# Feed-forward network in five 128-token tiles per pair of images instead of six, with the left-over tokens collected over pairs

## The chip, the cores and the metric

One Trainium2 chip, one of its cores. The metric is the device time of one execution in microseconds (us), the median of several runs. Engines are called as the profile calls them: PE (matmul), PEld (weight load of PE), DVE (vector), ACT (scalar), POOL (GpSimd), SP (which here only issues DMAs).

## What is computed

Thirty-two images of 224 x 224 x 3 go through a tokenizer, an attention block and a feed-forward network (FFN); all of it is float32 but the two matmuls of the FFN, whose operands are rounded numbers held exactly in bf16. Cut to what matters here:

```python
# tokenizer: two embeddings of 16x16 patches, five depthwise 3x3 convolutions with a pointwise one
# each, layer norm; 196 tokens an image, one class token before, 128 text tokens behind: T = 325
h = concat([cls, layernorm(tokenizer(x)), txt], axis=1)      # 32 x 325 x 192
# attention: q, k, v are small MLPs of layernorm(h), a query sees the 64 keys before it
h = h + layernorm(scores @ v)
# FFN, token by token (D = 192, H = 512)
t = layernorm(h)
u, g = split(bitlinear(t, w_in, g_in))                       # 192 -> 2 x 512
out = h + bitlinear(gelu(g) * u, w_out, g_out)               # 512 -> 192
# bitlinear(x): rmsnorm, scale by the row's maximum, round, multiply by weights of -1, 0, 1
```

Everything behind the attention works on a token by itself, so it does not matter there which tokens share a tile of 128 partitions.

## The kernel before, in words

The work goes in 16 pairs of images. An image has 325 tokens, held in three tiles of 128, 128 and 69 rows (`ROWS`); a pair has `NT` = 6 tiles, and row n of the list `(0..2)` is the first image, `(3..5)` the second. Each engine has one function `turn(it, par, on)`, which is an order written out by hand: for turn `it` it issues one piece of the youngest pair's embedding, pieces of the older pairs' convolutions, attention and FFN, up to six pairs deep. `all_turns` calls it for 22 turns. So in the steady state a turn of each engine holds the work of one pair, taken from five or six different pairs, and the only thing that sets the order of an engine is its `turn`.

The pieces that matter here:

- `embed_chunk(pair, m, ks)` (L389 inside) multiplies x by the weights, 18 float32 matmuls of 392 columns a pair. SP's `load_x` brings the next pair's x when the last one has been used.
- `square` (L367 to L372) and `mlp` (L419 to L424) are the pointwise convolutions and the six projections' matmuls.
- `transposes(a, t)` (L431) turns the normalised tokens of tile t of both images, packed side by side in `xh`, into columns `xT`: three PE transposes a tile.
- `mixed_values(a, i)` (L472 to L478) makes the attention's output, three units a pair. Unit 1 is the third tile (69 rows) of the two images: four matmuls of 192 columns, two for each image.
- The FFN of a tile n of pair f: `round_tokens` (ACT), `rounded_token_transposes` (PE, L491, 2 transposes), `rounded_tokens` (ACT), `ffn_in` (PE, L501, 4 bf16 matmuls of 512 columns), `gate_tanh` (ACT), `gated` and `lifted` (DVE, L1383 and L1402), `hidden_scale` (POOL), `mean_square` (ACT), `hidden_root` (POOL), `hidden_round` (DVE, L1161 to L1174), `round_hidden` (ACT), `rounded_hidden_transposes` (PE, L513, 4 transposes), `rounded_hidden` (ACT), `ffn_out` (PE, L522, 4 bf16 matmuls of 192 columns), `finished` (DVE, L1392), `store` (SP). There is one buffer for nearly all of it, so tiles follow each other through a chain of engines.
- Before the first tile of a pair, `hidden_bn` (L1316), `token_scale_0` to `token_scale_3` and `token_gain` on DVE make the scales of all six tiles at once.

A float32 matmul is two PE instructions in the trace (the two passes follow each other), a transpose or a bf16 matmul is one.

## Time and profile before

| | |
|---|---|
| median of 3 runs | 1230.72 us (1226.99 to 1232.67) |
| the profiled execution | 1227.0 us, its span 1225.1 us |
| mean granted clock of TensorE | 0.959 of full speed |
| busy: PE, PEld | 1122.0 us (92%), 853.2 us |
| busy: DVE, ACT, POOL | 1038.1 us (85%), 966.7 us (79%), 813.9 us (66%) |
| DMA | 40.25 MB, 9.2% of the 16 engines' time |
| PE's share of the chain that ended last | 81% |

The page of the profile gives, for each group of instructions, the busy time, the mean of one, and how long the engine stood idle before it and for whom. Its second part cuts the span in 40 slices: PE is busy in all but the first four and the last eight or so, and the granted clock is full (9) until the last two. The page's averages are taken over stages with different limits, so the prediction reads stretches of the time line.

### The profile page before, as it was taken

Reading aid. Unit: us, or ns where it says so; the run is one execution under the profiler, and the core shown is the slowest. Engines: PE = TensorE matmul, PEld = TensorE weight load, DVE = VectorE, ACT = ScalarE, POOL = GpSimd, SP = SyncE. Lnnn points to the kernel's source line nnn. Section 1 sums busy time; section 2 is a strip of 40 time slices with the busy share of each in tenths; the row PEclk is TensorE's granted clock in tenths of the full one; section 3 lists DMA queues with packets and bytes.
Section 4 is the critical chain, followed back from the end, with each engine's and each line's share of the span. In section 5 each row is a group of like instructions: output and inputs, shape, how many; then the busy total and the mean of one; then the engine's idle time right before and its main releaser. Section 6 shows DMA issues by size and latency. Waiting matters only on the chain.

```text
span 1225.1 us, 19501 instructions
## 1 busy us (share of the span) xinstructions
PE 1122.0 (92%) x5617; PEld 853.2 (70%) x5674; DVE 1038.1 (85%) x3012; ACT 966.7 (79%) x2437; POOL 813.9 (66%) x860
## 2 busy tenths in 40 slices
PE   6777999999999999999999999999999998889544
PEld 3555777777777777777777777777877766566322
DVE  1887598999999999999999999999999998866643
ACT  4556677989898988979898989889798978776543
POOL 4454576776877867777768778677777686755421
PEclk9998999999999999999999999999999999999655
DMA  8111010101010010101010100101010000000000
GB/s 320 40 47 40 8 40 7 49 14 49 5 49 15 16 49 15 49 12 49 13 50 5 45 19 16 49 15 49 12 49 13 11 6 19 6 19 11 12 11 10
DMA packets 21513, 40.25 MB, mean 33 GB/s; under 512 B 2656, under 2 KB 18208, under 8 KB 19104
## 3 DMA queue, kind: packets, MB, share of 16 engines
q1 hardware_dynamic: 21408, 39.01, 9.2%
q8 instruction: 46, 0.75, 0.3%
q14 instruction: 59, 0.48, 0.1%
HBM read 31.02 MB, written 7.99 MB: 32 GB/s over the span
## 4 chain that ended last, share of the span: by engine, by line
PE 81%; ACT 6%; DVE 6%; POOL 4%; issue 2%; DMA 1%; SPq 0%; DVEq 0%; POOLq 0%; ACTq 0%
PE bank L389 14%; PE bank L419 6%; PE bank L420 6%; PE bank L501 6%; PE bank L367 4%; PE bank L368 4%; PE bank L422 3%; PE bank L424 3%; PE bank L423 3%; PE bank L513 3%; PE bank L522 3%; PE bank L443 2%; PE bank L444 2%; PE bank L370 2%; PE bank L371 2%
## 5 line engine op out<-in xcount | busy, mean ns | idle before, releaser
L1212 DVE SCALAR_TENSOR_TENSOR bank<-padA,c_col,bank 128x406 f32<-128x406 f32 x560 | 357.8, 639 | 7.8
L389 PE MATMUL bank<-x_sb,w_emb 128*128 128x392 f32 x576 | 215.3, 500 | 11.4 <-ACT padA L746 7.3
L801 ACT ACTIVATE prod<-padB,c_col 128x196 f32<-128x196 f32 x432 | 181.3, 448 | 33.9 <-DVE padB L1233 31.1
L1692 POOL TENSOR_TENSOR yg<-y_f,c_gout 128x512 f32<-128x512 f32 (+1 forms) x96 | 121.8, 1268 | 109.8 <-DVE y_f L1402 109.8
L389 PEld LDWEIGHTS bank<-x_sb,w_emb 128*128 128x128 f32 x576 | 102.8, 191 | 63.7 <-ACT padA L746 9.2
L801 ACT ACTIVATE early<-padB,c_col 128x196 f32<-128x196 f32 x288 | 124.1, 452 | 1.9 <-POOL accB L1723 1.4
L1685 POOL TENSOR_TENSOR s<-s,c_mhalf 128x1 f32<-128x1 f32 (+1 forms) x96 | 53.0, 552 | 84.3 <-ACT s L877 84.3
L1383 DVE SCALAR_TENSOR_TENSOR ya<-th,bank 128x512 f32<-128x512 f32 (+1 forms) x96 | 65.6, 683 | 48.7 <-ACT th L870 48.1
L501 PE MATMUL bank<-w_in,xq 128*128 128x512 bf16 (+1 forms) x327 | 93.3, 404 | 8.7 <-ACT xq L864 5.7
L858 ACT ACTIVATE yq<-bank 128x512 bf16<-128x512 f32 (+1 forms) x96 | 50.8, 530 | 56.9 <-PE bank L513 56.5
L870 ACT ACTIVATE th<-bank,sm 128x512 f32<-128x512 f32 (+1 forms) x96 | 65.4, 681 | 24.7 <-PE bank L501 24.0
L513 PE MATMUL bank<-c_id,r 128*128 128x128 f32 (+1 forms) x384 | 56.3, 273 | 29.0 <-DVE y_f L1402 26.4
L1392 DVE SCALAR_TENSOR_TENSOR o_sb<-bank,dq,h 128x192 f32<-128x192 f32 (+1 forms) x96 | 39.6, 412 | 44.4 <-PE bank L522 44.4
L367 PE MATMUL bank<-accA,w_sq 128*128 128x196 f32 x256 | 65.9, 339 | 11.6 <-DVE accA L1212 5.3
L501 PEld LDWEIGHTS bank<-w_in,xq 128*128 128x128 bf16 (+1 forms) x384 | 39.4, 105 | 52.9 <-issue 16.5
L513 PEld LDWEIGHTS bank<-c_id,r 128*128 128x128 f32 (+1 forms) x384 | 44.6, 150 | 43.4 <-ACT r L850 37.3
L850 ACT ACTIVATE r<-yg,s 128x512 f32<-128x512 f32 (+1 forms) x96 | 68.7, 716 | 5.1 <-DVE s L1174 4.5
L864 ACT ACTIVATE xq<-bank 128x256 bf16<-128x256 f32 (+1 forms) x96 | 34.0, 354 | 45.8 <-PE bank L491 44.5
L419 PE MATMUL bank<-xT,w_sq 128*128 128x325 f32 x192 | 68.9, 440 | 0.7 <-ACT xT L760 0.7
L420 PE MATMUL bank<-xT,w_sq 128*128 128x325 f32 x192 | 68.2, 436 | 0.0
L1708 POOL TENSOR_TENSOR prod<-prod 128x392 f32<-128x392 f32 x48 | 48.8, 1017 | 29.0 <-ACT prod L801 29.0
L1685 POOL TENSOR_TENSOR sm<-sm,c_mhalf 128x6 f32<-128x6 f32 x32 | 43.7, 1366 | 36.0 <-DVE sm L1358 35.2
(224 smaller groups left out, 3461.2 us busy)
## 6 DMA issues: line engine op xcount, KB each, us to landing
x_sb<-xt SPq DMA_DIRECT2D x16, 1176.0 KB, 5.4
out<-o_sb SPq DMA_DIRECT2D x64, 96.0 KB
w_sq<-squares SPq DMA_DIRECT2D x1, 3840.0 KB, 16.4
h_sb<-txt SPq DMA_DIRECT2D x32, 51.8 KB
out<-o_sb SPq DMA_DIRECT2D x32, 51.8 KB
h_sb<-txt SPq DMA_DIRECT2D x32, 44.2 KB
w_in<-win SPq DMA_DIRECT2D x1, 1024.0 KB, 18.1
c_row<-broads SPq DMA_DIRECT2D x1, 672.0 KB, 19.2
```

Source lines behind the costliest of these rows:

```text
L367: mm(dstA[img], w[:, AA, :], chunks[img], start=True, stop=False)
L389: done = mm(pE[:, 0:2 * N_PATCH], w_emb[:, k, m, :], x_sb[:, k, :], start=k == 0, stop=k == KC - 1)
L419: mm(dst, w[:, AA, :], src[:, c, :], start=True, stop=False)
L420: mm(dst, w[:, B0A + c, :], src[:, 2, :], start=False, stop=True).then_inc(at_full, 1)
L501: done = mm(dst[0:m, :], xq[:, c, 0:m], w_in[:, c, half * HID:(half + 1) * HID], start=c == 0, stop=c == 1)
L513: done = nc.tensor.transpose(pUP[:, c * P:c * P + m], r2[0:m, c * P:(c + 1) * P], c_id[0:m, 0:m])
L801: made = go(grid(prod[ACC[s] ^ 1][:, k, :]), tap_view(padB[min(s, 2)], SIDE, k), ACT.Copy, scale=tapcol(s, 1, k))
L850: go(r2[0:m, :], yg[0:m, :], ACT.Copy, scale=s2[0:m, 6:7], bias=MAGIC).then_inc(r2_ready, 1)
L1212: v.scalar_tensor_tensor(grid(acc if k == TAPS - 1 else run), tap_view(pad, ROWS_A, k), tapcol(s, 0, k), grid(run), ALU.mult, ALU.add).the ...
L1383: v.scalar_tensor_tensor(ya[0:m, :], th[0:m, :], 1.0, pGT[0:m, :], ALU.add, ALU.mult).then_inc(f_y, 1)
L1685: return g.tensor_tensor(ap, ap, c_mhalf[0:m, 0:n], ALU.pow)
L1692: g.tensor_tensor(yg[0:m, :], y_f[0:m, :], c_gout[0:m, :], ALU.mult).then_inc(f_yg, 1)
```

## The change

Of an image's 325 tokens, 256 fill two tiles, 64 more go into one half of a third tile that the two images of a pair share (tile 2), and 5 are left. So a pair has five FFN tiles of 128 rows and 10 tokens left over. These 10 rows of `h2` are copied by two DMAs a pair (`hold`) into a side tile `h_side`, which is run through the FFN as a sixth tile of pair 11 (120 rows, pairs 0 to 11) and of pair 15 (40 rows, pairs 12 to 15). FFN tiles: 96 before, 82 after.

```diff
+FFN_TILES = 5
+SIDE_PAIRS = (11, PAIRS - 1)
+LEFT = T - 2 * P - DB
+HELD = 2 * LEFT
+TOK_ROWS = [P] * 5 + [DB + LEFT]
...
+def n_tiles(pair):
+    return FFN_TILES + side(pair)
+def tile_no(pair, n):
+    return pair * FFN_TILES + (pair > SIDE_PAIRS[0]) + n
+def rows(pair, n):
+    return P if n < FFN_TILES else HELD * len(members(group(pair)))
...
 # SP: store of a tile
+                if n == FFN_TILES:
+                    for i, pair in enumerate(members(group(f))):
+                        for img in range(2):
+                            lo = i * HELD + img * LEFT
+                            sp.dma_start(out[pair * 2 + img, T - LEFT:T, :], at[lo:lo + LEFT, :]).then_inc(done, 16)
+                elif n == 2:
+                    for img in range(2):
+                        sp.dma_start(out[f * 2 + img, 2 * P:2 * P + DB, :],
+                                     at[img * DB:(img + 1) * DB, :]).then_inc(done, 16)
...
+            def hold(f, par):
+                sp.wait_ge(h2_ready, f + 1)
+                lo = (f - members(group(f))[0]) * HELD
+                for img in range(2):
+                    sp.dma_start(h_side[group(f)][lo + img * LEFT:lo + (img + 1) * LEFT, :],
+                                 h2[par][img * DB:img * DB + LEFT, TILES + 2, :]).then_inc(held[f % 2], 16)
...
 # PE: the transposes of the third tiles
+            def tail_transposes(a):
+                both = pT[(U_XT + 2) % 2][:, 0:2 * P].rearrange("p (i n) -> p i n", i=2)
+                feat = pT[(U_XT + 2) % 2][:, 2 * P:3 * P]
+                pick = c_id[0:TOK_ROWS[5], :].rearrange("p (i n) -> p i n", i=2)[:, :, 0:LEFT]
+                mm(both[:, :, 0:DB], xh[:, 2, 0:P], c_id[:, :].rearrange("p (i n) -> p i n", i=2), start=True, stop=True)
+                mm(both[:, :, DB:DB + LEFT], xh[0:TOK_ROWS[5], 2, D:D + P], pick, start=True, stop=True)
+                for img in range(2):
+                    o = slice(img * DB, (img + 1) * DB)
+                    mm(feat[o, 0:DB], xh[:, 2, P:D], c_id[:, o], start=True, stop=True)
+                for img in range(2):
+                    o = slice(img * DB, (img + 1) * DB)
+                    done = mm(feat[o, DB:DB + LEFT], xh[0:TOK_ROWS[5], 2, D + P:2 * D],
+                              c_id[0:TOK_ROWS[5], img * DB:img * DB + LEFT], start=True, stop=True)
...
 # PE: unit 1 of the mixed values
+                if i == 1:
+                    half = [slice(img * DB, (img + 1) * DB) for img in range(2)]
+                    for img in range(2):
+                        mm(pT[u % 2][half[img], 0:D], sc1[:, img, P:P + DB], v_sb[:, 1, img, :], start=True, stop=False)
+                    for img in range(2):
+                        mm(pT[u % 2][half[img], 0:D], sc2[0:n2, img, 0:DB], v_sb[0:n2, 2, img, :], start=False, stop=True)
+                    for img in range(2):
+                        done = mm(pT[u % 2][img * DB:img * DB + LEFT, D:2 * D], sc2[0:n2, img, DB:DB + LEFT],
+                                  v_sb[0:n2, 2, img, :], start=True, stop=True)
-                    else:
-                        mm(dst, sc2[0:n2, img, :], v_sb[0:n2, 2, img, :], start=True, stop=False)
-                        done = mm(dst, sc1[:, img, P:P + n2], v_sb[:, 1, img, :], start=False, stop=True)
...
 # DVE: the scales of a pair; with a side tile they wait for the copies
+                if tiles[-1] == NT - 1 and side(f):
+                    for p in range(2):
+                        dve.wait_ge(held[p], (f + 1) // 2 * 32)
...
 # POOL: h2 is not written before it was copied
+                    pool.wait_ge(held[f % 2], f // 2 * 32)
```

The text tokens are loaded with six DMAs a pair instead of four (64 of them go into tile 2, 5 into tile 5). Every step that counted tiles as `f * NT + n` counts them as `tile_no(f, n)`. And the `turn` functions of all five engines are written in a new order; the functions they call are the same, with `if side(...)` around the steps of a sixth tile. Three places of it follow.

PE, one steady turn: the mixed values (L472 to L478) and the transposes of the third tiles (the last L431 row). Before:

```order
L491 MATMUL bank<-c_id,r 128x69 x2
L389 MATMUL bank<-x_sb,w_emb 128x392 x2
L501 MATMUL bank<-w_in,xq 69x512 x4
L477 MATMUL bank<-v_sb,sc 69x192
L478 MATMUL bank<-v_sb,sc 69x192
L477 MATMUL bank<-v_sb,sc 69x192
L478 MATMUL bank<-v_sb,sc 69x192
...
L431 MATMUL bank<-c_id,xh 128x128 x3
L522 MATMUL bank<-w_out,yq 128x192 x4
L431 MATMUL bank<-c_id,xh 128x69 x3
```

And of the change, the same stretch:

```order
L595 MATMUL bank<-c_id,r 128x128 x2
L568 MATMUL bank<-v_sb,sc 64x192 x2
L570 MATMUL bank<-v_sb,sc 64x192 x2
L572 MATMUL bank<-v_sb,sc 5x192 x2
L605 MATMUL bank<-w_in,xq 128x512 x4
...
L527 MATMUL bank<-c_id,xh 128x128 x3
L508 MATMUL bank<-c_id,xh 128x2x64
L509 MATMUL bank<-c_id,xh 128x2x5
L512 MATMUL bank<-c_id,xh 64x64 x2
L515 MATMUL bank<-c_id,xh 64x5 x2
```

Four matmuls of 69 output rows have become six, of 64, 64 and 5 rows, and three transposes have become six matmuls.

DVE, the second pair at the program's start: the last taps of its convolution F1 (L1212) and the statistics of the first pair's tokens (L1270), before:

```order
L1212 SCALAR_TENSOR_TENSOR bank0<-padA2,c_col,bank0 128x406 x6
L1270 BN_STATS st_a<-h_sb 128x6 x2
L1270 BN_STATS st_a<-h_sb 69x6
L1270 BN_STATS st_a<-h_sb 128x6 x2
L1270 BN_STATS st_a<-h_sb 69x6
```

```order
L1315 SCALAR_TENSOR_TENSOR bank0<-padA2,c_col,bank0 128x406 x5
L1315 SCALAR_TENSOR_TENSOR accA0<-padA2,c_col,bank0 128x406
L1373 BN_STATS st_a<-h_sb 128x6 x5
L1373 BN_STATS st_a<-h_sb 69x6
```

The last tap, which writes `accA0` for PE, stood behind the statistics and now stands ahead of them.

SP, the end of its queue of the change (before, it ends with six stores of one DMA each for every pair):

```order
L380 DMA h_side<-h_1 5x192 x2
L373 DMA out<-o_sb 128x192
L369 DMA out<-o_sb 64x192 x2
L373 DMA out<-o_sb 128x192 x4
L369 DMA out<-o_sb 64x192 x2
L373 DMA out<-o_sb 128x192 x2
L366 DMA out<-o_sb 5x192 x8
```

The two copies of the last pair stand ahead of its stores, and the last store is eight DMAs of five rows.

## Rows read from the trace of the kernel before

**Rows 1.** busy time of each engine in stretches (columns: stretch; its us; busy us, instructions)

```profile
105.00:172.00 67.00, 67.00 (x318) 53.41 (x317) 47.77 (x113) 47.21 (x122) 34.55 (x41) 0.99 0.12 40
...
914.70:982.00 67.30, 67.09 (x350) 52.17 (x353) 63.32 (x187) 59.39 (x151) 49.95 (x53) 1.00 0.04 11
982.00:1049.60 67.60, 59.04 (x312) 44.40 (x314) 60.77 (x187) 56.81 (x141) 50.35 (x50) 1.00 0.04 12
1170.00:1225.00 55.00, 25.85 (x89) 11.86 (x88) 19.42 (x55) 21.05 (x48) 10.86 (x12) 0.50 0.03 10
```

**Rows 2.** time line of PE, FFN tiles in a steady turn (start us; busy us; instruction)

```profile
638.64 0.41 PE L513 MATMUL bank<-c_id,r 69*128 69x69 f32 x4
638.89 0.76 PE L422 MATMUL bank<-xT,w_sq 128*128 128x325 f32 x2
...
657.54 0.29 PE L491 MATMUL bank<-c_id,r 69*128 69x69 f32 x2
657.67 0.76 PE L419 MATMUL bank<-hq,w_sq 128*128 128x325 f32 x2
...
658.82 1.02 PE L501 MATMUL bank<-w_in,xq 128*69 128x512 bf16 x4
659.68 0.71 PE L422 MATMUL bank<-hq,w_sq 128*128 128x325 f32 x2
...
666.06 0.60 PE L513 MATMUL bank<-c_id,r 128*128 128x128 f32 x4
666.49 0.71 PE L419 MATMUL bank<-hk,w_sq 128*128 128x325 f32 x2
...
667.59 0.49 PE L522 MATMUL bank<-w_out,yq 128*128 128x192 bf16 x4
667.92 1.51 PE L389 MATMUL bank<-x_sb,w_emb 128*128 128x392 f32 x4
669.27 0.38 PE L491 MATMUL bank<-c_id,r 128*128 128x128 f32 x2
669.49 0.71 PE L422 MATMUL bank<-hk,w_sq 128*128 128x325 f32 x2
```

**Rows 3.** the same time line: mixed values unit 1, transposes, narrow matmuls

```profile
683.08 0.29 PE L457 MATMUL bank<-q,k 128*69 128x69 f32 x2
683.21 0.54 PE L456 MATMUL bank<-q,k 128*128 128x191 f32 x2
...
690.27 0.49 PE L477 MATMUL bank<-v_sb,sc 69*69 69x192 f32 x2
...
691.58 0.49 PE L472 MATMUL bank<-v_sb,sc 128*128 128x192 f32 x2
...
698.93 0.35 PE L431 MATMUL bank<-c_id,xh 69*128 69x69 f32 x3
699.12 1.53 PE L389 MATMUL bank<-x_sb,w_emb 128*128 128x392 f32 x4
```

**Rows 4.** time line at the start, DVE

```profile
99.24 1.65 DVE L1270 BATCH_NORM_STATS2 st_a<-h_sb 128x6 f32<-128x192 f32 x6 [4.91 <-DMA h_sb<-cls]
...
101.73 0.63 DVE L1212 SCALAR_TENSOR_TENSOR accA<-padA,c_col,bank 128x406 f32<-128x406 f32 x1
```

**Rows 5.** time line at the start, PE

```profile
102.46 0.99 PE L367 MATMUL bank<-accA,w_sq 128*128 128x196 f32 x2 [3.32 <-DVE accA L1212]
```

**Rows 6.** time line of the end: DVE's statistics of pairs 13 and 15

```profile
1047.86 1.65 DVE L1316 BATCH_NORM_STATS2 st_f<-h 128x6 f32<-128x192 f32 x6
...
1156.39 1.66 DVE L1316 BATCH_NORM_STATS2 st_f<-h 128x6 f32<-128x192 f32 x6 [0.98 <-POOL h L1751]
```

**Rows 7.** line 1392 on DVE (ns min/median/max, first and last start us, forms)

```profile
L1392 DVE SCALAR_TENSOR_TENSOR o_sb<-bank,dq,h x96: 403/415/420, 215.0 to 1222.2; 128x192 f32<-128x192 f32 x64, 69x192 f32<-69x192 f32 x32
```

**Rows 8.** SP's issues of line 320 (ns min/median/max, first and last start us)

```profile
L320 SPq DMA_DIRECT2D h_sb<-txt x6: 362/705/2042, 607.4 to 743.0; - x6
```

**Rows 9.** the page's DMA issues (KB each, median us to landing)

```profile
x_sb<-xt SPq DMA_DIRECT2D x16, 1176.0 KB, 5.4
```

More of the change, by code:

```diff
@@ L151, in build @@
         sm = [sb(f"sm{i}", [P, 12, NT]) for i in range(2)]
+        h_side = [sb(f"h_side{i}", [P, D]) for i in range(2)]
         w_g = sb("w_g", [P, NT, D])
@@ L329, in turn @@
             def turn(it, par, on):
+                if on[6]:
+                    store(it - 6, 3)
+                    if side(it - 6):
+                        store(it - 6, 4)
+                if on[3]:
+                    load_cls(it - 3)
+                if on[6]:
+                    store(it - 6, n_tiles(it - 6) - 1)
+                if on[5]:
+                    store(it - 5, 0)
                 if on[0]:
@@ L494, in ffn_in @@
             def ffn_in(f, n):
-                m = ROWS[n % TILES]
-                pe.wait_ge(f_xq, f * NT + n + 1)
-                if not (first(f) and n < 2):
-                    pe.wait_ge(f_yq, f * NT + n - 1)
+                m = rows(f, n)
+                pe.wait_ge(f_xq, tile_no(f, n) + 1)
+                if not (tile_no(f, n) < 2):
+                    pe.wait_ge(f_yq, tile_no(f, n) - 1)
                 for half, dst in ((0, pUP), (1, pGT)):
@@ L516, in ffn_out @@
             def ffn_out(f, n):
-                m = ROWS[n % TILES]
-                pe.wait_ge(f_yq, f * NT + n + 1)
-                if not (first(f) and n == 0):
-                    pe.wait_ge(f_out, f * NT + n)
+                m = rows(f, n)
+                pe.wait_ge(f_yq, tile_no(f, n) + 1)
+                if not (tile_no(f, n) == 0):
+                    pe.wait_ge(f_out, tile_no(f, n))
                 for c in range(4):
@@ L607, in turn @@
                     ffn_out(it - 5, 0)
+                if on[1]:
+                    embed_chunk(it - 1, EMB_GA, range(4, 6))
                 if on[4]:
@@ new lines, in turn @@
+                if on[5]:
+                    if side(it - 5):
+                        round_tokens(it - 5, odd, 5)
+                    rounded_tokens(it - 5, 4)
+                if on[1]:
+                    products(it - 1, L_, range(7, 8))
+                    products(it - 1, L_, range(8, 9))
+                    mix_out(it - 1)
+                if on[3]:
+                    mlp_out(it - 3, U_K1, hk, "kb1", ACT.Gelu, 1)
+                if on[5]:
+                    gate_tanh(it - 5, 4, odd)
@@ new lines, in turn @@
+                if on[3]:
+                    mlp_out(it - 3, U_V1, hv, "vb1", ACT.Gelu, 1)
+                if on[2]:
+                    products(it - 2, F3_, range(1, 2))
+                    products(it - 2, F3_, range(2, 3))
+                if on[3]:
+                    mlp_out(it - 3, U_V1, hv, "vb1", ACT.Gelu, 2)
+                if on[2]:
+                    products(it - 2, F3_, range(3, 4))
+                    products(it - 2, F3_, range(4, 5))
+                if on[5]:
+                    if side(it - 5):
+                        rounded_tokens(it - 5, 5)
@@ new lines, in turn @@
+                if on[3]:
+                    queries_out(it - 3, 1)
+                if on[5]:
+                    if side(it - 5):
+                        rounded_hidden(it - 5, 4)
+                if on[1]:
+                    loc_out(it - 1)
+                if on[4]:
+                    round_tokens(it - 4, par, 1)
+                    rounded_tokens(it - 4, 0)
+                if on[3]:
+                    queries_out(it - 3, 2)
+                if on[0]:
+                    products(it, G_, range(3, 4))
@@ L1313, in hidden_bn @@
                     dve.wait_ge(h2_ready, f + 1)
-                for n in tiles:
-                    m = ROWS[n % TILES]
-                    done = v.bn_stats(st_f[0:m, n, :], h2[par][0:m, n, :])
+                if tiles[-1] == NT - 1 and side(f):
+                    for p in range(2):
+                        dve.wait_ge(held[p], (f + 1) // 2 * 32)
+                for n in range(tiles[0], min(tiles[-1] + 1, n_tiles(f))):
+                    m = rows(f, n)
+                    done = v.bn_stats(st_f[0:m, n, :], hidden(f, par, n))
                 if tiles[-1] == NT - 1:
@@ new lines, in turn @@
+                if on[2]:
+                    taps(it - 2, F3_, 3)
+                if on[5]:
+                    if side(it - 5):
+                        lifted(it - 5, 5)
+                if on[2]:
+                    taps(it - 2, F3_, 4)
+                if on[1]:
+                    if first(it - 1):
+                        ternary_weights()
+                if on[2]:
+                    taps(it - 2, F3_, 5)
+                    taps(it - 2, F3_, 6)
+                if on[5]:
+                    hidden_round(0, it - 5, n_tiles(it - 5) - 1, odd)
```

1071 lines of the change are left out of this document (524 added, 547 removed).

## The prediction

> **What bounds the kernel now.** I read the stretches first, then single pieces of PE's time line, then the two ends. From 105 us on PE is busy in every microsecond: 67.00 of 67.00 us, and still 67.09 of 67.30 us before 982 us, at the full granted clock, 1.00, which is the 2.4 GHz level [rows 1]. In the same stretches DVE, the next engine, has 63.32 of 67.30 us to do [rows 1]. One turn of the program, the work of one pair, takes some 67.4 us here. So for 877 us, 13 turns, the time is the number of microseconds that PE streams, and what DVE, ACT and POOL save is worth nothing. Behind 982 us this ends: PE has 59.04 and DVE 60.77 of 67.60 us, and in the last 55 us PE works 25.85 us at a granted clock of 0.50, the 1.2 GHz level [rows 1]: only FFN tiles are left, one after the other. There, and at the start, waits decide. The change has to be priced by these two rules: PE's streaming in the middle, the chain at the ends.
>
> **FFN tiles on PE.** The price of a piece is the start of what follows it less its own start, since matmuls overlap by their tails. A 128-row tile: hidden transposes 666.49 - 666.06 = 0.43 us, output matmuls 0.33, token transposes 0.22 [rows 2], and input matmuls 659.68 - 658.82 = 0.86 us, which have 512 columns however many rows the tile has. Together 1.84 us. A 69-row tile: 0.25 + 0.33 (the same 192 columns) + 0.13 + 0.86 = 1.57 us [rows 2]. A pair had 4 x 1.84 + 2 x 1.57 = 10.50 us and has 5 x 1.84 = 9.20 us: **-1.30 us a turn**. A sixth of the tiles goes, but only an eighth of their PE time, and what goes were the cheap ones. FFN tiles run from 215 us on (DVE's first `finished` [rows 7]), so up to 982 us this is worth 767 / 67.4 = 11.4 turns, -14.8 us. The side tile of pair 11 stands where that pair's sixth tile stood, with 120 rows for 69: +0.3 us, in the stretch where PE is no longer full; I leave it out.
>
> **Mixed values, unit 1.** Four matmuls of 192 columns take 691.58 - 690.27 = 1.31 us, 0.327 us each, of two passes [rows 3]. Now there are six, because each image's 69 queries are cut in 64 and 5, and a matmul of 5 output rows streams the same 192 columns. The rows show that 69 or 128 output rows make no difference and that each float32 matmul starts when the one before has streamed; by that six cost 1.96 us, **+0.65 us a turn**. Below, the two matmuls of each couple write different partitions (0 to 63, 64 to 127); if they streamed wholly side by side, the unit would cost 3 x 0.327 = 0.98 us, -0.33. I take +0.65, the value that the rows show, and keep the other end for the range. 13 turns: +8.5 us.
>
> The Trainium skill speaks for the other end: "TensorE: Matmul & The Clock Gate", Part 3 on packing small matmuls, has three matmuls with 32 output rows each on column tiles of their own run 2.38 times as fast as one after the other. Nothing in this trace uses such tiles. It is my first rival.
>
> **Transposes of the third tiles.** Three transposes of 69 columns, one pass each, take 699.12 - 698.93 = 0.19 us [rows 3]. They become six ordinary float32 matmuls, two passes each: one of 128 columns (a pass of 128 columns is 0.11 us, half of the two token transposes [rows 2]), 0.22 us; one of 10; two of 64; two of 5. A 69-column matmul costs 683.21 - 683.08 = 0.13 us for two passes [rows 3]. Four passes of 64 columns are thus 0.24 us. The six passes of 5 or 10 columns cost between 0.04 us (by their columns) and 0.39 us (as much as 69 columns, if loading the weights sets a least time); the nearest row is a 69-column pass, so I take 0.38. Sum 0.84 us, **+0.65 us a turn** (from +0.3), 13 turns: +8.4 us.
>
> So in the middle the change gives -14.8 + 8.5 + 8.4 = **+2.1 us**: what the FFN saves on PE, the attention's pieces pay back.
>
> **The start.** The last tap of the second pair's convolution F1 now stands ahead of the statistics on DVE. Before, it was queued behind them, they waited 4.91 us for a DMA, and PE waited 3.32 us for the tap [rows 4, 5]. That wait goes. What is late next are the transposes that need those statistics, which had hidden behind F1's matmuls. Bounds 0 and -3.3 us; I take -2.0 us. The rest of DVE's order at the start is the same.
>
> **The end.** From pair 13's statistics to pair 15's are 1156.39 - 1047.86 = 108.5 us for two pairs, 54.3 us a pair [rows 6], with 12 FFN tiles in them. If the FFN's chain alone set this, a tile would be worth 9.0 us; if the last pair's attention does, nothing. Pairs 12, 13 and 14 each lose a tile. DVE's share (60.77 of 67.60 us [rows 1]) says that both are near; I take a third, 2.7 us a tile, **-8 us**. Pair 15 keeps six tiles. Against that stand: pair 15's own unit 1 and transposes, now on the chain, +1.3 us; its side tile's statistics wait for `h2`, an SP issue and a landing, where the sixth tile's `h2` was ready, +0.8 us; and the last store is eight DMAs where it was one. SP needs 0.36 us for an issue at the least [rows 8], so seven more are 2.5 us, of which part lies beside the first ones' landing: +2.0 us. Net -3.9 us (from -20 to +4). The 24 DMAs of the first side tile (some 9 us of SP) come behind 982 us, with no x left to load; I cost them at nothing, their cover being the one tile that may pass before `o_sb` is needed again.
>
> Nothing is taken for the two copies a pair, the two more text loads (DMA's share is under a tenth), or for the work saved on DVE, ACT and POOL in the middle: PE's streaming covers it all.
>
> **Sum:** +2.1 - 2.0 - 3.9 = -3.8 us against the profiled execution's 1227.0 us, so 1223.2 us. That execution is at the low end of the runs; the median is 3.7 us above it, and I put the change's median as much above its own: **1226.9 us**. A measurement of this kernel tells about 0.5%, 6.2 us, from no change: faster is below 1224.6, slower above 1236.9.
>
> **Rivals.**
> *The couples stream together (faster).* Within a couple the second matmul's first pass can run beside the first matmul's second pass, and so on through the unit: 12 passes of 0.163 us take the time of 7, 0.82 us less a turn; in the transposes 8 narrow passes take the time of 5, 0.18 us less. 13 turns: -13.0 us, 1213.9 us. For it: the couples are written next to each other, image by image, onto different partitions. Against: nothing in this trace does it, and between their two passes they are in one order.
> *A change of the array's shape stops PE (slower).* The program has only full-width matmuls now. The change brings in widths of 64 and 32 output rows. If PE must finish one width before it starts the next, each change shows the tail that is hidden today: a float32 couple of passes is busy 0.49 us where the next starts after 0.33 [rows 3], so 0.16 us. Three changes in unit 1 and two in the transposes make 0.8 us a turn, 13 turns +10.4 us: 1237.3 us; if the weight load is not hidden either, up to 10 us more. It decides from 0.1 us a change on. The Trainium skill states this rule: "TensorEngine Tiling (Array Packing)", Key Properties, says that changing the tiling mode drains TensorE. No row of this trace shows it.
> *Both at once:* 1226.9 - 13.0 + 10.4 = 1224.3 us.
> *The new order makes PE wait for x (slower).* Behind the last use of a pair's x, PE now has the transposes of a third tile, G and W2 (14 matmuls of 196 columns, 0.33 us each), four of 325 columns (0.55 each) and half an FFN tile, some 9 us, before it needs the next pair's x; before, some five projections' pieces more stood between. The load lands 5.4 us after its issue [rows 9], so it holds unless SP is late by over 3 us behind a store. If each turn lost 1 us: 1240 us.
>
> **How the numbers follow.** Forecast as summed 0.28, together 0.25, both 0.17, shape alone 0.20, a wait in the new order 0.10. Each case spreads by some 6 us, by the end's bounds above all. Faster by over 0.5%: 0.10 + 0.24 + 0.09 = 0.43. Slower: 0.01 + 0.01 + 0.13 + 0.05 = 0.20. The rest, 0.37, within. The range goes from the first rival less 2 us, 1212, to the shape rival plus 5 us, 1242. The likeliest case alone spans 1220 to 1233.
>
> **What would show it.** PE stays full from 105 us to 982 us, with a turn of 67.5 us (forecast), 66.5 (together), 68.3 (shape). Unit 1's starts: 1.96 us to the next piece, or 1.14; gaps of 0.16 us and more ahead of the first 64-row and the first 128-row matmul for the shape rival. The third transposes: 0.84 us. Pair 13 to pair 15 in some 103 us. From DVE's last `finished` (start 1222.2 before [rows 7], the span's end 2.9 us later) to the end some 5 us. I am wrong if PE shows idle time in the middle, or if the end moves by more than 8 us.

## The result, and the profile after

| | before | after |
|---|---|---|
| median | 1231.53 us (4 runs, 1226.99 to 1232.67) | 1209.33 us (4 runs, 1208.73 to 1211.12) |
| ratio | | 0.9829, 95% interval 0.9801 to 0.9857 |
| profiled execution, span | 1227.0, 1225.1 us | 1211.1, 1209.3 us |
| mean granted clock | 0.959 | 0.952 |
| busy PE, PEld | 1122.0, 853.2 us | 1117.2, 843.2 us |
| busy DVE, ACT, POOL | 1038.1, 966.7, 813.9 us | 990.9, 926.1, 786.5 us |
| DMA | 40.25 MB | 40.36 MB |

The change is 1.7% faster. I had forecast 1226.9 us and a range of 1212 to 1242: the time lies below the range, and 4.6 us below my fastest rival. The stretches of the changed kernel, columns as in [rows 1]:

```profile
105.00:172.00 67.00, 66.94 (x333) 52.44 (x332) 49.05 (x115) 46.88 (x121) 33.87 (x37) 0.99 0.11 40
914.70:982.00 67.30, 67.11 (x367) 52.80 (x366) 63.74 (x185) 57.88 (x148) 50.06 (x52) 1.00 0.04 12
982.00:1049.60 67.60, 60.64 (x320) 45.45 (x319) 56.63 (x179) 53.06 (x130) 44.67 (x46) 0.95 0.04 13
1170.00:1209.30 39.30, 16.52 (x59) 7.74 (x58) 13.07 (x37) 13.68 (x30) 7.23 (x8) 0.50 0.04 11
```

Up to 982 us PE is as full as before: the middle is still PE's. So the question is how long a turn is. A good clock for that is SP's load of x, once a pair: SP issues it when PE has read the last of the pair's x. That place is not the same in the two orders, so what lies ahead of the sixth load and behind the last one can shift by some us from one to the other; the length of ten turns can't. The sixth and the last load (start us, us) of the kernel before:

```profile
228.54 0.35 SPq L304 DMA_DIRECT2D x_sb<-xt  x1
...
903.05 0.35 SPq L304 DMA_DIRECT2D x_sb<-xt  x1
```

and of the changed kernel:

```profile
227.91 0.35 SPq L356 DMA_DIRECT2D x_sb<-xt  x1
...
892.51 0.34 SPq L356 DMA_DIRECT2D x_sb<-xt  x1
```

Ten turns took 674.51 us and take 664.60: 67.45 and 66.46 us each. Against the kernel before, the changed one has gained 0.6 us up to the sixth load, 9.9 us in the ten turns, and 5.3 us from the last load to the end (322.05 and 316.79 us): 15.8 us in all, the difference of the spans. The 0.6 us is understated: up to 60 us this execution had a granted clock of 0.91, the kernel before 0.97. Experiments 3, 6 and 11, whose kernels differ from the changed one there only in a few matmuls of a turn, had 0.97 and their sixth load at 224.8 to 225.6 us, some 3 us ahead of the kernel before.

On PE's time line, a steady turn, unit 1 of the mixed values (L568 to L572) and the third tiles' transposes (L508 to L515) read:

```profile
616.04 0.38 PE L595 MATMUL bank<-c_id,r 128*128 128x128 f32 x2
616.35 0.55 PE L568 MATMUL bank<-v_sb,sc 128*64 128x192 f32 x4
616.73 0.50 PE L570 MATMUL bank<-v_sb,sc 69*64 69x192 f32 x4
617.16 0.50 PE L572 MATMUL bank<-v_sb,sc 69*5 69x192 f32 x4
617.59 1.04 PE L605 MATMUL bank<-w_in,xq 128*128 128x512 bf16 x4
...
627.14 0.39 PE L508 MATMUL bank<-c_id,xh 128*128 128x128 f32 x2
627.36 0.29 PE L509 MATMUL bank<-c_id,xh 69*128 69x10 f32 x2
627.58 0.34 PE L512 MATMUL bank<-c_id,xh 128*64 128x64 f32 x4
627.74 0.24 PE L515 MATMUL bank<-c_id,xh 69*64 69x5 f32 x4
627.91 0.44 PE L595 MATMUL bank<-c_id,r 128*128 128x128 f32 x2
628.18 0.50 PE L444 MATMUL bank<-accA,w_sq 128*128 128x196 f32 x2
```

Unit 1's six matmuls, twelve passes, take 617.59 - 616.35 = 1.24 us, less than the four (eight passes) before took (1.31 us [rows 3]). I had 1.96. The transposes take 627.91 - 627.14 = 0.77 us; I had 0.84. The same unit in a window 0.06 us wide shows how the first couple begins:

```profile
616.15 0.27 PE L595 MATMUL bank<-c_id,r 128*128 128x128 f32 x1
616.35 0.38 PE L568 MATMUL bank<-v_sb,sc 128*64 128x192 f32 x2
```

Two passes stand in 0.38 us, which is what one lasts: they begin 7 ns apart, one for each image. The next two follow after 0.21 us, the later pairs after 0.16. And the two transposes of L595, 0.22 us elsewhere in the turn, hold PE for 616.35 - 616.04 = 0.31 us ahead of the 64-row matmuls and 628.18 - 627.91 = 0.27 us behind them: each change of width leaves a gap. Both of my rival mechanisms are there at once, the first stronger than I had it.

At the start the wait that I had struck out is still there, with another releaser (PE; before, it was 3.32 us for DVE's tap at 102.46 [rows 5]):

```profile
101.51 0.99 PE L444 MATMUL bank<-accA,w_sq 128*128 128x196 f32 x2 [3.79 <-POOL accB L1837]
```

At the end: DVE's statistics of the last pair, its last two finished tiles, and SP's last store.

```profile
1136.11 0.88 DVE L1422 BATCH_NORM_STATS2 st_f<-h 128x6 f32<-128x192 f32 x3 [1.05 <-POOL h L1867]
...
1200.16 0.42 DVE L1498 SCALAR_TENSOR_TENSOR o_sb<-bank,dq,h 128x192 f32<-128x192 f32 x1 [0.61 <-PE bank L626]
...
1203.84 0.41 DVE L1498 SCALAR_TENSOR_TENSOR o_sb<-bank,dq,h_side 40x192 f32<-40x192 f32 x1 [2.72 <-PE bank L626]
1204.27 2.93 SPq L366 DMA_DIRECT2D out<-o_sb  x8
```

The last finished tile starts 5.5 us ahead of the span's end, where it was 2.9 us [rows 7].

### The profile page after: what moved, and what is told of

Its sections match the earlier page's. It is cut to its first block, busy times and chain, and to the rows that moved or that the text cites. A ratio compares the mean times of both kernels' runs of the same rounds, so it can differ in the third digit from the quotient of the medians.

```text
span 1209.3 us, 19230 instructions
## 1 busy us (share of the span) xinstructions
PE 1117.2 (92%) x5686; PEld 843.2 (70%) x5686; DVE 990.9 (82%) x2844; ACT 926.1 (77%) x2309; POOL 786.5 (65%) x832
## 2 busy tenths in 40 slices
DMA packets 22983, 40.36 MB, mean 33 GB/s; under 512 B 3968, under 2 KB 19680, under 8 KB 20576
## 4 chain that ended last, share of the span: by engine, by line
PE 85%; DVE 5%; ACT 4%; POOL 2%; issue 1%; DMA 1%; SPq 0%; DVEq 0%; POOLq 0%
PE bank L466 15%; PE bank L496 7%; PE bank L497 7%; PE bank L605 6%; PE bank L444 4%; PE bank L445 4%; PE bank L499 3%; PE bank L501 3%; PE bank L500 3%; PE bank L617 3%; PE bank L539 3%; PE bank L626 2%; PE bank L540 2%; PE bank L552 2%; PE bank L553 2%; PE bank L447 2%
## 5 line engine op out<-in xcount | busy, mean ns | idle before, releaser
L1806 POOL TENSOR_TENSOR yg<-y_f,c_gout 128x512 f32<-128x512 f32 (+1 forms) x82 | 104.6, 1276 | 125.5 <-DVE y_f L1508 99.6
L605 PE MATMUL bank<-w_in,xq 128*128 128x512 bf16 (+2 forms) x328 | 93.0, 410 | 10.0 <-ACT xq L972 10.0
L1819 POOL TENSOR_TENSOR prod<-prod 128x392 f32<-128x392 f32 x48 | 49.2, 1026 | 45.9 <-ACT prod L909 45.9
L617 PE MATMUL bank<-c_id,r 128*128 128x128 f32 (+2 forms) x328 | 53.3, 289 | 25.6 <-DVE y_f L1508 21.4
L1498 DVE SCALAR_TENSOR_TENSOR o_sb<-bank,dq,h 128x192 f32<-128x192 f32 x80 | 33.3, 416 | 53.2 <-PE bank L626 53.1
L617 PEld LDWEIGHTS bank<-c_id,r 128*128 128x128 f32 (+2 forms) x328 | 41.3, 149 | 46.1 <-ACT r L958 30.1
L958 ACT ACTIVATE r<-yg,s 128x512 f32<-128x512 f32 (+1 forms) x82 | 58.9, 718 | 16.6 <-DVE s L1277 16.3
L1822 POOL TENSOR_TENSOR prod<-prod 128x392 f32<-128x392 f32 x48 | 48.9, 1019 | 34.2 <-ACT prod L909 34.1
L1857 POOL TENSOR_TENSOR y_sb<-y_sb,c_row 128x1152 f32<-128x1152 f32 x16 | 42.1, 2632 | 41.8 <-ACT y_sb L932 41.8
L1305 DVE TENSOR_SCALAR bank<-padA,c_col 128x406 f32<-128x406 f32 x80 | 51.0, 638 | 21.6 <-ACT padA L855 15.0
L605 PEld LDWEIGHTS bank<-w_in,xq 128*128 128x128 bf16 (+2 forms) x328 | 31.3, 102 | 52.3 <-issue 15.9
```

What stands on the lines that cost most here:

```text
L605: done = mm(dst[0:m, :], xq[:, c, 0:m], w_in[:, c, half * HID:(half + 1) * HID], start=c == 0, stop=c == 1)
L617: done = nc.tensor.transpose(pUP[:, c * P:c * P + m], r2[0:m, c * P:(c + 1) * P], c_id[0:m, 0:m])
L958: go(r2[0:m, :], yg[0:m, :], ACT.Copy, scale=s2[0:m, 6:7], bias=MAGIC).then_inc(r2_ready, 1)
L1806: g.tensor_tensor(yg[0:m, :], y_f[0:m, :], c_gout[0:m, :], ALU.mult).then_inc(f_yg, 1)
```

## The experiments

Twelve kernels ran. Ratios are to the kernel before, whose median was 1230.0 to 1231.3 us in these batches; the changed kernel stands at 0.9829.

**1. The order alone.** The kernel before, six tiles a pair, with the changed kernel's `turn` functions on all five engines and `if side(...)` always true. Of PE's, for instance:

```diff
-                if on[4]:
-                    values(it - 4, 0)
-                if on[6]:
-                    rounded_hidden_transposes(it - 6, 5)
+                if on[6]:
+                    rounded_hidden_transposes(it - 6, NT - 1)
+                if on[4]:
+                    values(it - 4, 0)
```

> The kernel before with the changed kernel's order of work on all five engines, and still six tiles a pair (256 + 69 rows an image): nothing of the computation is changed. Tiles theory (the time was gained by the fewer tiles and by couples that run side by side): only the start gains, 2 us as in the prediction, the turn stays at 67.45 us, the drain keeps its 18 tiles: ratio to before 0.998. Order theory (the new order took away small waits of PE, which I read as 0.35 us a turn, and tightened start and drain): turn 67.1 us, 13 x 0.35 = 4.5 us, with start and end 8 to 12 us less: ratio 0.990 to 0.993.

Measured: 1275.39 us, ratio 1.0363 (1.0349 to 1.0377), 44.6 us slower. Both theories missed. PE is no longer full (the stretch from 640 us on; then its longest waits in all, us in total, times, longest):

```profile
640.00:915.00 275.00, 264.89 (x1362) 200.98 (x1361) 244.38 (x726) 232.44 (x593) 195.02 (x201) 1.00 0.09 29
```

```profile
PE bank L493 <- DVE o_sb L1394: 29.0, 38, 2.3
PE bank L515 <- DVE y_f L1404: 27.6, 15, 3.1
```

L493 are the token transposes of a tile, which wait until the tile two before it is finished. In the stretch PE stands for 10.1 of the 275 us, 6.2 of them in this wait. A turn takes 70.85 us. I read it so: the new order leaves the FFN's chain room for five tiles a turn, and the sixth one comes too soon behind the others.

**2. The couples apart.** Unit 1 image by image:

```diff
                     for img in range(2):
                         mm(pT[u % 2][half[img], 0:D], sc1[:, img, P:P + DB], v_sb[:, 1, img, :], start=True, stop=False)
-                    for img in range(2):
                         mm(pT[u % 2][half[img], 0:D], sc2[0:n2, img, 0:DB], v_sb[0:n2, 2, img, :], start=False, stop=True)
```

> The changed kernel with the four 64-row matmuls of unit 1 of the mixed values issued image by image (both of the first image, then both of the second) instead of couple by couple. Forecast's rule (each float32 matmul starts when the one before has streamed): nothing changes, ratio to the changed kernel 1.000. Side by side, and issued in order: the passes are 0.163 us, the couples take 4 of them now; apart only the second pass of the first image's last matmul can run beside the second image's first, so 7: +3 x 0.163 = 0.49 us a turn, 16 turns +7.8 us, ratio to the changed kernel 1.0065, turn 66.95 us. Side by side, but with an own queue for each half of the array: nothing changes either, and the starts of the couple's passes stay 7 ns apart.

Measured: 1209.74 us, ratio 0.9827 (0.9814 to 0.9841), the turn 66.47 us. The program issues these four as

```
L568 MATMUL bank<-v_sb,sc 64x192
L569 MATMUL bank<-v_sb,sc 64x192
L568 MATMUL bank<-v_sb,sc 64x192
L569 MATMUL bank<-v_sb,sc 64x192
```

and the trace has both of L568 first, in a window 0.03 us wide and in the time line of the unit:

```profile
616.18 0.27 PE L594 MATMUL bank<-c_id,r 128*128 128x128 f32 x1
616.38 0.39 PE L568 MATMUL bank<-v_sb,sc 128*64 128x192 f32 x2
```

```profile
616.38 0.55 PE L568 MATMUL bank<-v_sb,sc 128*64 128x192 f32 x4
616.75 0.50 PE L569 MATMUL bank<-v_sb,sc 69*64 69x192 f32 x4
617.19 0.50 PE L571 MATMUL bank<-v_sb,sc 69*5 69x192 f32 x4
```

From L568 to L571 it takes 0.81 us, as in the changed kernel (616.35 to 617.16). The first passes of both images still begin together (now 14 ns apart), though a whole other matmul stands between them in the program. It looks as if each half ran from a queue of its own; the trace shows the starts, not the queues.

**3. Two more changes of width.**

```diff
                 mm(both[:, :, 0:DB], xh[:, 2, 0:P], ...)
-                mm(both[:, :, DB:DB + LEFT], xh[0:TOK_ROWS[5], 2, D:D + P], pick, start=True, stop=True)
                 for img in range(2):
                     mm(feat[o, 0:DB], xh[:, 2, P:D], c_id[:, o], start=True, stop=True)
+                mm(both[:, :, DB:DB + LEFT], xh[0:TOK_ROWS[5], 2, D:D + P], pick, start=True, stop=True)
```

> The changed kernel with the transposes of the third tiles in another order: the 128-row one, the 64-row couple, the other 128-row one, the narrow 64-row couple. The array's width now changes four times there instead of twice, the matmuls are the same. If a change of width costs nothing of its own: ratio to the changed kernel 1.000, turn 66.46 us. Shape theory (a change costs 0.10 to 0.16 us, the gaps I read in the trace of the changed kernel): +0.2 to +0.3 us a turn, turn 66.7 us, +3.2 to +5 us, ratio 1.003 to 1.004.

Measured: 1212.58 us, ratio 0.9858 (0.9838 to 0.9877), the turn 66.80 us. PE's time line:

```profile
626.91 0.39 PE L508 MATMUL bank<-c_id,xh 128*128 128x128 f32 x2
627.22 0.34 PE L511 MATMUL bank<-c_id,xh 128*64 128x64 f32 x4
627.49 0.39 PE L512 MATMUL bank<-c_id,xh 69*128 69x10 f32 x2
627.81 0.29 PE L515 MATMUL bank<-c_id,xh 69*64 69x5 f32 x4
628.02 0.44 PE L595 MATMUL bank<-c_id,r 128*128 128x128 f32 x2
```

1.11 us where it was 0.77: +0.34 us for two changes, 0.17 each, somewhat over my bound of 0.16. It shows that the change costs, not the matmuls, which are the same. The median is 3.3 us above the changed kernel's; 13 turns of 0.34 us would be 4.4. The two intervals overlap.

**4. The tap alone.** The kernel before with `taps(it - 1, F1_, 8)` ahead of `input_bn(it - 2, ...)`.

> The kernel before with one step moved: the last tap of convolution F1 stands ahead of the token statistics on DVE, as in the changed kernel. The prediction's term for the start: -2.0 us (0 to -3.3), ratio to before 0.998, and nothing in the middle, whose turn stays 67.45 us. Rival: the gained wait comes back as a wait of the transposes for the statistics: 1.000. Rival: the tap, now in time in every turn, also takes 0.1 us or more of a PE wait out of each turn: 0.997 or less.

Measured: 1232.15 us, ratio 1.0004 (0.9996 to 1.0013): nothing. PE at the same place:

```profile
103.69 0.99 PE L367 MATMUL bank<-accA,w_sq 128*128 128x196 f32 x2 [1.89 <-POOL accB L1722]
```

The tap's wait became POOL's: the second of the two operands (`accB`) comes from POOL. In the kernel before, its last write ended at 101.14 us and DVE's tap at 102.36, so at most 1.2 of the 3.32 us could go. The row itself can't price even these: PE's chunk ahead of it started 2.4 us later than before (98.82 against 96.43 us), in part at a lower granted clock (0.84 against 0.87 from 60 to 105 us). The medians of 11 and 15 executions leave no gain.

**5. Five tiles in the old order.** The changed kernel with the old `turn` functions; what stood for tile 5 stands for the last tile, and the sixth tile's own steps are run only where there is one. `hold` was put at the end of SP's turn:

```diff
+                    if side(it - 5):
+                        ffn_in(it - 5, 5)
 ...
                 if on[4]:
                     store(it - 4, 0)
+                if on[3]:
+                    hold(it - 3, 1 - par)
```

> The changed kernel's computation (five tiles a pair, side tiles, six matmuls in unit 1, six in the third tiles' transposes) in the order of the kernel before on all five engines; the steps of the sixth tile are left out where there is none, nothing is moved to fill their place. Tiles theory: by PE's ledger the tiles, unit 1 and the transposes are worth -1.15 - 0.07 + 0.59 = -0.63 us a turn, so a turn of 66.8 us, 13 x 0.63 = -8.2 us, and three tiles less in the drain, -8 us by the prediction's third of a tile: ratio to before 0.985 to 0.989. Order theory (the new order is fitted to five tiles, the old one to six, as e1_order_only showed the other way round with +3 us a turn): with five tiles the old order has a hole, PE waits, turn 67.3 us or more and ratio 0.992 or more.

Measured: 1314.11 us, ratio 1.0682 (1.0655 to 1.0709). A miss for both, and my own doing, as SP's queue and PE show:

```profile
624.86 1.53 SPq L380 DMA_DIRECT2D h_side<-h  x2
626.44 0.44 SPq L356 DMA_DIRECT2D x_sb<-xt  x1
...
632.14 2.98 PE L465 MATMUL bank<-x_sb,w_emb 128*128 128x392 f32 x4 [4.87 <-DMA x_sb<-xt]
```

The copies wait for `h2`, the load of x stands behind them, and PE waits 4.87 us for x; it does so twelve times in the run, 4.2 to 4.9 us each. It is my rival on x in the flesh: in the changed kernel the copies stand behind the load.

**6. Without the last side tile.** `side(pair)` is true for pair 11 only.

> The changed kernel without the side tile of the last pair: the last 5 tokens of the images of pairs 12 to 15 (40 rows) get no FFN and are not stored. Chain theory: what goes is the last step of the chain (last but one finished tile to the last, 3.7 us) and the seven more DMAs of the last store (5.5 us from the last finished tile to the end, where one DMA takes 2.9 us), -6.3 us, and some 0.8 us for the statistics that wait for the copies: ratio to the changed kernel 0.994 to 0.995. Rival, a tile costs its whole turn through the chain as the full ones do, 8.5 us, and the store's 2.6 us: -11 us, 0.991.

Measured: 1198.28 us, ratio 0.9736 (0.9717 to 0.9755), 11 us less than the changed kernel: the rival's price. In the profiles 7.2 us of it lie between the last statistics and the last finished tile (67.7 and 60.5 us), 2.9 us behind that. So a tile of 40 rows costs 7.2 us, nearly as much as any in the drain, and my "+0.8 us" for it was the step of one wait in place of a tile.

**7. One width in unit 1.**

```diff
-        sc2 = sb("sc2", [P, 2, ROWS[2]])
+        sc2 = sb("sc2", [P, 2, P])
-                        done = mm(pT[u % 2][img * DB:img * DB + LEFT, D:2 * D], sc2[0:n2, img, DB:DB + LEFT],
+                        done = mm(pT[u % 2][half[img], D:2 * D], sc2[0:n2, img, DB:2 * DB],
```

> The changed kernel with the two 5-row matmuls of unit 1 made 64 rows wide (59 columns of zeros more in sc2), so that unit 1 uses one width instead of two. Shape theory: one change of width less a turn, 0.10 us by the gap ahead of the 5-row matmuls: unit 1 takes 1.14 instead of 1.24 us, turn 66.36 us, 16 x 0.10 = -1.6 us, ratio to the changed kernel 0.9987. Rival (the gap belongs to the narrow matmuls, not to the change of width): the gap moves or stays, 1.000. If zeros had to be streamed at a price of their own: slower.

Measured: 1208.64 us, ratio 0.9820 (0.9801 to 0.9840), the turn 66.35 us, unit 1 1.13 us:

```profile
614.86 0.55 PE L568 MATMUL bank<-v_sb,sc 128*64 128x192 f32 x4
615.24 0.50 PE L570 MATMUL bank<-v_sb,sc 69*64 69x192 f32 x4
615.56 0.49 PE L572 MATMUL bank<-v_sb,sc 69*64 69x192 f32 x4
615.99 1.04 PE L605 MATMUL bank<-w_in,xq 128*128 128x512 bf16 x4
```

The gap ahead of the last couple is gone (0.32 us from L570 to L572, was 0.43). By the turn the shape theory holds; its 1.6 us are too little for the medians, 0.7 us apart, to show.

**8. One DMA for a side tile's store.**

```diff
-                    for i, pair in enumerate(members(group(f))):
-                        for img in range(2):
-                            sp.dma_start(out[pair * 2 + img, T - LEFT:T, :], at[lo:lo + LEFT, :]).then_inc(done, 16)
+                    imgs = members(group(f))
+                    sp.dma_start(out[2 * imgs[0]:2 * imgs[-1] + 2, T - LEFT:T, :], at[0:rows(f, n), :]).then_inc(done, 16)
```

> The changed kernel with each side tile's store as one DMA of 40 (first side tile 120) rows instead of 8 (24) DMAs of 5 rows. Issue theory (the prediction's term, seven issues of 0.36 us by SP): -2.0 to -2.6 us, the end 2.9 to 3.3 us behind the last finished tile instead of 5.5, ratio to the changed kernel 0.998. Rival (many short rows land slowly however they are issued): 1.000, the end stays 5 us or more behind. The wait of 1.0 us of DVE for the first side tile's stores behind 1003 us goes too, without a price.

Measured: 1205.92 us, ratio 0.9802 (0.9782 to 0.9822). SP's store takes 0.74 us, and the span (1204.1 us) ends 2.9 us behind the last finished tile:

```profile
1201.21 0.41 DVE L1497 SCALAR_TENSOR_TENSOR o_sb<-bank,dq,h_side 40x192 f32<-40x192 f32 x1 [2.72 <-PE bank L625]
1201.65 0.74 SPq L364 DMA_DIRECT2D out<-o_sb  x1
```

**9. Five tiles in the old order, the copies behind x**, those of pairs 11 and 15 still at the turn's end.

> As e5_tiles_only, the five tiles in the order of the kernel before, but the two copies to the side tile no longer stand ahead of the load of x on SP: they come behind it, and only the two pairs with a side tile are copied at the turn's end. In e5_tiles_only the load was issued 1.58 us behind the copies, which waited for h2, and PE waited 4.9 us for x in most turns of 73.4 us. SP theory: that wait was most of the loss, the turn falls by 5 us or more to 67 to 68.5 us, ratio to before 0.99 to 1.00. Order theory (the hole of the missing sixth tile makes PE wait for the FFN's chain whatever SP does): PE's waits for y_f, r and yq stay, the turn stays above 69 us, ratio 1.02 or more. Tiles theory as before: 66.8 us, 0.985.

Measured: 1234.27 us, ratio 1.0045 (1.0025 to 1.0065). PE is full (400.00 of 400 us from 400 to 800 us), the turn 66.62 us, but for one of 83.7 us around pair 11's copies: SP's queue was the loss in the middle. But the whole is 0.4% slower than before.

**10. Both images on one half.**

```diff
-                        mm(pT[u % 2][half[img], 0:D], sc1[:, img, P:P + DB], ...)
+                        mm(pT[u % 2][0:DB, img * D:(img + 1) * D], sc1[:, img, P:P + DB], ...)
```

> The changed kernel with all six matmuls of unit 1 writing partitions 0 to 63 (the second image's result goes to other columns of the same partitions): same matmuls, same widths, same three changes of width, but both images on one half of the array. It leaves the second image's third tile in the wrong place. Side by side theory (what ran two at a time were the two halves): 12 passes of 0.163 us one after the other, 1.96 us for 0.98 us, unit 1 from 1.24 to 2.2 us, turn 67.4 us, 16 turns +15 us, ratio to the changed kernel 1.011 to 1.013. Rival (a 64-row matmul simply streams faster, half the rows at half the price): nothing changes, turn 66.46 us, 1.000.

Measured: 1224.32 us, ratio 0.9958 (0.9941 to 0.9975), the turn 67.42 us, 15.0 us over the changed kernel.

```profile
622.21 0.54 PE L569 MATMUL bank<-v_sb,sc 128*64 128x192 f32 x2
622.59 0.49 PE L570 MATMUL bank<-v_sb,sc 69*64 69x192 f32 x2
622.92 0.49 PE L569 MATMUL bank<-v_sb,sc 128*64 128x192 f32 x2
623.24 0.49 PE L570 MATMUL bank<-v_sb,sc 69*64 69x192 f32 x2
623.66 0.81 PE L572 MATMUL bank<-v_sb,sc 69*5 69x192 f32 x4
624.41 1.04 PE L605 MATMUL bank<-w_in,xq 128*128 128x512 bf16 x4
```

2.20 us for the same six matmuls of the same widths. What my forecast assumed of unit 1 is true on one half: 12 passes of 0.163 us one after the other are its 1.96 us, and the rest are the gaps between widths.

**11. Experiments 7 and 8 together.**

> The changed kernel with the edits of e7_wide_left (the 5-row matmuls made 64 rows wide) and of e8_one_store (one DMA for a side tile's store) together. They act at different places, so the gains should add: turn 66.36 us and the end 2.9 us behind the last finished tile, -0.7 to -1.6 and -2.6 to -3.4 us, 1205.0 us, ratio to before 0.979. Rival: the gain of the middle is eaten by the drain, as it is PE's there no more: as e8_one_store, 1205.9 us.

Measured: 1204.31 us, ratio 0.9807 (0.9777 to 0.9838), turn 66.35 us. The best median of the kernels that do the whole work, 5.0 us under the changed kernel, though it can't be told from experiment 8.

**12. Five tiles in the old order, all copies behind x.**

> As e9_tiles_held, but the copies to the side tile stand behind the load of x in every turn, as in the changed kernel; the one turn of 83.7 us (loads of x at 832.6 and 916.2 us) should then be 66.6 us like the others, and the statistics of pairs 11 and 12 66.6 us apart instead of 73.4. Middle term: turn 66.62 us as in e9_tiles_held, 10 turns -8.3 us against before. Drain theory (with the old order a missing tile in the drain is worth nothing, the last pairs' attention sets it, as 170.1 us from pair 12 to pair 15 in e9_tiles_held against 169.8 before says): 1234.3 - 6.8 = 1227.5 us, ratio to before 0.997. Prediction's drain term (2.7 us for each of three tiles): 0.990. The rest to the changed kernel, 0.983, would be the order's.

Measured: 1232.83 us, ratio 1.0005 (0.9985 to 1.0024), the turn 66.62 us. All turns with a load of x are even now. Of the 6.8 us that I had added up, 1.4 us came by the medians and some 5 by the two ratios; against the kernel before nothing is gained. The twelve executions spread from 1223.2 to 1237.2 us: the five with a mean granted clock of 0.955 and more took 1229.3 us or less, the seven with 0.952 and less 1232.3 or more. The profiled one (1233.4 us, 0.952) is one of the seven. Here the loads of x are at

```profile
233.53 0.34 SPq L356 DMA_DIRECT2D x_sb<-xt  x1
...
899.73 0.34 SPq L356 DMA_DIRECT2D x_sb<-xt  x1
```

and the table below puts the four kernels of order and tiles side by side (us; a pair's `h2` is the start of its statistics on DVE).

| | before | order alone (1) | tiles alone (12) | changed |
|---|---|---|---|---|
| tiles a pair, order | six, old | six, new | five, old | five, new |
| median | 1231 | 1275 | 1233 | 1209 |
| sixth load of x | 228.5 | 227.1 | 233.5 | 227.9 |
| a turn | 67.45 | 70.85 | 66.62 | 66.46 |
| last load of x to pair 15's `h2` | 253.3 | 262.5 | 259.2 | 243.6 |
| of it: up to pair 11's `h2` | 16.1 | 9.6 | 16.2 | 9.4 |
| of it: pair 11's to pair 15's `h2` | 237.2 | 252.9 | 243.0 | 234.2 |
| from pair 15's `h2` to the end | 68.7 | 75.3 | 72.6 | 73.2 |

Fewer tiles in the new order are worth 66 us, in the old one nothing that the spread shows; the new order with six tiles costs 44 us, with five it saves 24. Neither part of the change gains anything without the other. The tiles alone do gain 8.3 us in ten turns, but they lose 5.0 ahead of the sixth load and 9.8 behind the last one. Why they lose at the start stays open. In the drain one row shows a loss. The last pair's first token transposes, in the kernel before, with the tiles alone, and in the changed kernel:

```profile
1168.51 0.66 PE L491 MATMUL bank<-c_id,r 128*128 128x128 f32 x2 [0.60 <-DVE o_sb L1392]
```

```profile
1171.18 0.69 PE L594 MATMUL bank<-c_id,r 128*128 128x128 f32 x2 [10.45 <-ACT r L950]
```

```profile
1149.79 0.69 PE L595 MATMUL bank<-c_id,r 128*128 128x128 f32 x2 [2.68 <-ACT r L952]
```

With the old order PE has nothing left while the last pair's attention runs out, and stands 10.45 us. Before, the sixth tile of the pair before (its token transposes at 1159.73 us) filled that time. The new order spreads the five tiles so that 2.68 us are left.

## Why the prediction was wrong, point by point

**The bound.** Right: PE stayed full to 982 us, and the turn decided the middle. Here the turn of 66.46 us is the one that I had named for "together" (66.5), in part by luck: the couples gave less with their gaps than that rival had (unit 1 takes 1.24 us, not 1.14), and terms that I had at nothing made it up (see the middle's sum). For the profiled executions my sum was 12.1 us too high (1223.2 against 1211.1 us): some 8 us are unit 1, some 5 those terms at nothing, and the misses at the start and the end, 1.4 us each, cancel.

**FFN tiles, -1.30 us a turn.** Right as far as it went. Tokens 0.22, input 0.86, hidden 0.44 and output 0.33 us a tile give 1.85 us, 9.24 a turn, where the six took 10.52: -1.28. What I left out is the joint behind a 69-row tile's short transposes: the float32 matmul behind them holds PE 0.05 us longer than elsewhere, four times a turn. These 0.20 us went too.

**Unit 1, +0.65: the step that failed.** "The rows show ... that each float32 matmul starts when the one before has streamed; by that six cost 1.96 us". The rows of a full-width array can't show that, and I carried it to a half-width one. Measured: 1.24 us and a gap of 0.09 us ahead, so +0.02 us. Over 13 turns that is 8 us. Experiment 10 settles it: 2.20 us when both images use one half, +15.0 us in the time; experiment 2 shows that the order of issue does not matter. My rival had the right mechanism and nearly its size: 12 passes as 7, staggered, in a single queue. They go as 6.
The Trainium skill, "TensorE: Matmul & The Clock Gate", Part 3 (packed small matmuls, 2.38 times as fast for three of 32 rows), agrees: two of 64 rows go twice as fast here, or 2.20 / 1.24 = 1.8 times with the gaps between widths. The same part also has all matmuls start strictly in program order; issued image by image they would then take seven passes' time instead of four, and experiment 2 shows four. There the measurement decides.

**The third tiles' transposes, +0.65.** Right in sum (+0.58, and 0.05 us behind them), but not by its parts. The narrow passes of L515 take 0.17 us as a group, couples side by side, and two changes of width are in the rest.

**The shape rival.** Its mechanism is real: 0.09 to 0.10 us for each of the three changes in unit 1 and 0.17 for each one added in the transposes (experiments 3 and 7), some 0.6 us a turn if the two there cost the same. It is contained in the lengths above. The Trainium skill, "TensorEngine Tiling (Array Packing)", Key Properties, states that a change of mode drains TensorE; the trace agrees, and gives it these prices. "Both at once", 1224.3 us, was the right story, mis-sized on the gaining side.

**The middle's sum.** By the pieces (-1.28, +0.02 and +0.63 us) the turn should be 0.63 us shorter; it is 0.83 in the old order and 0.99 in the new one. The rest lies in joints, places outside these pieces where PE begins an instruction 0.02 us or more later than is usual for the shape before it: 0.55 us a turn before, 0.35 in experiment 12, 0.17 now, which closes both sums within 0.02 us. The largest share are the 0.20 us behind the 69-row tiles' transposes. Of the 0.16 us between the two orders with five tiles, some 0.15 lie behind the changes of width, where experiment 12 has a float32 matmul held by 0.10 us twice a turn and the changed kernel only once, by 0.05. So little is left open here, and less than 0.2 us a turn is the order's.

**The start, -2.0.** Wrong: experiment 4 gives 0. I named the transposes as what is late next; it was POOL's `accB`, which the same product needs and which I had not looked up. What the changed kernel is ahead at the sixth load (0.6 us in its profiled execution, some 3 us at the granted clock of the kernel before) lies elsewhere in the new order. No run took it apart.

**The end, -3.9.** The size was near (-5.3 us in the profiles) by luck, the reasons were not. "I take a third, 2.7 us a tile" has no single value: with the new order the last load of x to pair 15's `h2` fell by 18.9 us for three tiles and what they delayed (262.5 to 243.6), of which 4.5 us are the turn from pair 11 to pair 12 (71.0 and 66.5 us): some 5 us a tile; with the old one it rose by 5.9. Against the kernel before, pair 13 to pair 15 fell from 108.5 to 104.9 us; I had said some 103. I priced the tiles as if the order of the drain were given, while the change rewrites it. The last store, +2.0: right in kind, 2.6 us by experiment 8. Pair 15's side tile: "+0.8 us" for its wait; dropping the whole tile is worth 7.2 us.

**The order, not priced.** This is the largest omission. I took the new `turn` functions as a place where waits may arise (1240 us if so), never as something that the tiles need. The four kernels show that the change is one thing: five tiles a pair, and room for exactly five in the order.

**From profile to median.** I set the change's median 3.7 us above its profiled execution, as before. It lies 1.8 us below: the profiled execution was the fastest of four before and the slowest of four after, in part by the clock of its start. These 5.5 us decide that the time lies outside the range, not which way it went. And I gave each case a spread of 6 us but took only 2 us off the first rival (1213.9 us) for the range; 6 us would have held 1209.3.

Still open: which moves of the order carry the 15.6 us between 259.2 and 243.6. The table places them: 6.8 us are there before the drain, as pair 11's `h2` comes 9.4 instead of 16.2 us behind the last load, and 8.8 us lie between pair 11's and pair 15's `h2`, where the wait of 10.45 us fell to 2.68. It wasn't tried move by move.

## What to carry to other kernels

Here float32 matmuls of at most 64 output rows that write different halves of the partitions cost half, in both orders of issue that were tried, and a change of width cost 0.09 to 0.17 us: so cut work into couples, and group them. When work leaves a pipeline whose order is written by hand, price the order with it: fewer steps in an unchanged order may gain nothing, and a DMA that waits ahead of a load on one queue can cost more than all of it. Before striking out a wait, look up every operand of the waiting instruction.

## What was not expected of the hardware

The two halves of the array take their matmuls side by side, and not strictly in the program's order: in experiment 2 the second image's first pass began 14 ns behind the first image's, past another matmul of the first image. A 5-row matmul of 192 columns costs as much as a 64-row one (0.16 us a couple of passes in experiment 7 and in the changed kernel alike); only its own width costs, 0.10 us a turn. Eight DMAs of five rows put the end 2.6 us later than one DMA of forty. The granted clock of the first 60 us was 0.91 to 0.97 in the profiled executions of kernels in the new order, and with it the sixth load of x moved by 3 us: 227.9 us in the changed kernel and experiment 2 (0.91), 227.0 and 227.1 in 7 and 8 (0.94), 224.8 to 225.6 in 3, 6 and 11 (0.97).
